# A decoder layer's gate projection, computed inside the scan loops, kept in DRAM and reloaded

## The reference

```
xz = norm(x) @ W_in ; xp, z = split(xz)          # 512 + 512 channels
xc = silu(causal_conv(xp)) ; B, C = split(xc @ W_x) ; dt = softplus(xc @ W_dt + b)
h  = exp(dt * A) * h + dt * xc * B               # 16 states per channel
y  = sum over states (h * C) + D * xc
x  = x + (y * silu(z)) @ W_out                   # then attention, then experts
```

## Time and profile before

| what | value |
|---|---|
| median of 3 runs | 1635.24 us (1632.82 to 1635.37) |
| profiled execution, own time | 1633.4 us |
| its span | 1631.4 us |
| VectorE busy | 1405.1 us (86%) |
| TensorE busy | 1249.2 us (77%), weight loads 834.0 |
| GpSimd busy | 969.0 us (59%) |
| ScalarE busy | 931.2 us (57%) |
| mean granted TensorE clock | 0.891 |

### The profile page before, as it was taken

How to read it: one execution, slowest core, us unless ns; L and a number is a source line. 1 busy time by engine, 2 the same in 40 slices (tenths; PEclk the granted TensorE clock), 3 DMA queues, 4 the chain that set the end, 5 groups by cost and what they waited for, 6 DMA issues and landing times. The chain is left out here.

```text
span 1631.4 us, 22872 instructions
## 1 busy us (share of the span) xinstructions
PE 1249.2 (77%) x5502; PEld 834.0 (51%) x5558; DVE 1405.1 (86%) x1861; ACT 931.2 (57%) x1369; POOL 969.0 (59%) x529
## 2 busy tenths in 40 slices
PE   4766667898677767889777687898777677797797
PEld 2344444664455445565445455566345455565465
DVE  6599999796899999787799999888699999963687
ACT  2554444146777777334777767523777767612564
POOL 1399888213888889322798889430689888620000
PEclk9877787999798989999799989999789988997699
DMA  7111110202111111201111121021111111010111
GB/s 228 41 39 43 42 45 20 99 1 80 34 58 52 46 57 53 64 26 54 59 40 58 40 71 51 27 69 54 40 41 57 58 52 60 18 61 27 45 60 52
DMA packets 54633, 86.48 MB, mean 53 GB/s; under 512 B 8572, under 2 KB 35589, under 8 KB 54542
## 3 DMA queue, kind: packets, MB, share of 16 engines
q1 hardware_dynamic: 50972, 83.20, 15.3%
q10 hardware_dynamic: 3570, 2.21, 0.5%
HBM read 74.83 MB, written 10.57 MB: 52 GB/s over the span
## 5 line engine op out<-in xcount | busy, mean ns | idle before, releaser
L1692 PE MATMUL ps<-ident,work 128*128 128x128 f32 x1536 | 309.2, 324 | 247.6 <-DVE stage L1334 170.1
L1296 DVE TENSOR_TENSOR_SCAN work<-ps,work 128x1024 f32<-128x1024 f32 x192 | 438.3, 2283 | 18.1 <-ACT ps L917 10.2
L1692 PEld LDWEIGHTS ps<-ident,work 128*128 128x128 f32 x1536 | 188.5, 159 | 383.6 <-DVE stage L1334 221.6
L917 ACT ACTIVATE ps<-dt,a_neg 128x1024 f32<-128x1024 f32 x256 | 284.8, 1117 | 121.1 <-DVE work L1296 96.3
L672 POOL TENSOR_TENSOR work<-dtu,b_bc 128x1024 f32<-128x1024 f32 x128 | 299.1, 2365 | 46.8 <-PE ps L1692 43.0
L1334 DVE SCALAR_TENSOR_TENSOR stage<-ps,c_tok,stage 128x512 f32<-128x512 f32 x384 | 272.1, 733 | 22.2 <-PE ps L1692 19.7
L1714 PE MATMUL ps<-w,work 128*128 (+1 forms) x1024 | 269.5, 411 | 1.8 <-DVE work L1441 1.8
L1714 PEld LDWEIGHTS ps<-w,work 128*128 128x128 f32 x1024 | 216.3, 213 | 52.6 <-issue 10.2
L1664 PE MATMUL ps<-nfT,w 128*128 128x512 bf16 x456 | 155.1, 430 | 40.5 <-DVE work L1371 14.6
L672 POOL TENSOR_TENSOR work<-dtu,w_out 128x1024 f32<-128x1024 f32 x64 | 149.3, 2355 | 50.1 <-PE ps L1692 50.1
L688 POOL TENSOR_TENSOR stage<-stage,work 128x512 f32<-128x512 f32 x128 | 160.5, 1277 | 11.4 <-ACT work L933 11.4
(11 more groups left out here) (164 smaller groups left out, 1879.7 us busy)
## 6 DMA issues: line engine op xcount, KB each, us to landing
b_bc<-b_rows SPq DMA_DIRECT2D x32, 512.0 KB, 3.7
w_out<-b_rows SPq DMA_DIRECT2D x32, 512.0 KB, 3.9
wbc<-combine_rows SPq DMA_DIRECT2D x64, 256.0 KB, 3.3
stage<-in_x SPq DMA_DIRECT2D x8, 512.0 KB, 4.1
xt<-in_x SPq DMA_DIRECT2D x8, 512.0 KB, 5.8
x_rows<-xt SPq DMA_DIRECT2D x4, 1024.0 KB, 4.2
res<-x_rows SPq DMA_DIRECT2D x8, 512.0 KB, 4.0
out_x<-res SPq DMA_DIRECT2D x8, 512.0 KB, 3.3
```

The source lines that it names most:

```text
L917: act.activation(decay_in(d, alone, opening), dt[:, d, :], ACT.Exp, scale=a_neg[:, bass.ds(it * 2 + (d * N + hf * (N // 2) + par), 1)]).th ...
L1296: dve.tensor_tensor_scan(h, decays, h, 0.0, ALU.mult, ALU.add).then_inc(scan_done, 1)
L1692: mm = pe.transpose(ps[:, a % HT_BANKS, d * P:(d + 1) * P], slot(par, d)[:, a * P:(a + 1) * P], ident[:, :])
```

## The change

- Z products move from the head into the scan loops: one per two states (`z_product`: 128 tokens, 8 matmuls into bank 0 after tile 6 is accumulated; the second state of each pair in the first eight states, the first state of each pair in the last eight). ScalarE copies the result to SBUF (`keep_z`), SP stores it to a DRAM tensor `zd` (`store_z`). In loops with experts the copy lands in `mix`.
- When state 14 is transposed, SP loads both halves back (`load_head`) into `soft`, where the slots of state 14 were.
- ScalarE's second linear relu goes behind the next state's first decay in the states that keep a Z (`late_linear`). The second down product goes into the state after (`late_down`).
- At the end of a row the accumulates, gates, Y transposes, skips and gated products are interleaved, and the second finalize stands partly among them (`gate`, `skip`, `gated_product`). ScalarE stores the second half of the output.
- In state 9 the finalize moves behind scan 1 and behind scan 2. Its three adds become scalar_tensor_tensor with a multiplication by 1.
- PSUM banks of the jobs are listed by hand (`banks_of`), GpSimd's gated products move to the end of its loop, and the key bias is loaded after the last Y is taken. `phase_after(b)` is the phase that follows loop b.

The diff, cut to its core (indentation shortened by eight columns):

```diff
...
+def z_job(b, hf, it):
+    return b * TT + hf * ITS + it
...
     def phases(ph):
         r, b = ph.c_row, ph.a_row
         if r is not None:
-            wait_apart(sp, dbu_ready, (r + 1) * (N * CT) + DBU_CREDIT)
-            wait_apart(sp, hT_ready, (r + 1) * (N * TT) + HT_READY_CREDIT)
-            sp.dma_start(w_out[:, :, :].rearrange("p k n -> p (k n)"), w_outd).then_inc(w_out_loaded, 16)
-            load_x(r, xt, [xt_loaded, xt_loaded])
-            sp.dma_start(key_bias.rearrange("p (o f) -> p o f", o=1),
-                         k_rowd[bass.ds(r, 1), :].partition_broadcast(P)).then_inc(key_bias_loaded, 16)
             sp.dma_start(kq[:, :, :], kqd[bass.ds(r * P, P), :].rearrange("p (k f) -> p k f", k=DK)
                          ).then_inc(kv_loaded, 16)
             sp.dma_start(vo[:, :, :], vod[bass.ds(r * KEYS, KEYS), :].rearrange("p (k f) -> p k f", k=2)
...
+            ph.wait_taken(sp, ("Y", CT - 1, NH - 1))
+            sp.dma_start(key_bias.rearrange("p (o f) -> p o f", o=1),
+                         k_rowd[bass.ds(r, 1), :].partition_broadcast(P)).then_inc(key_bias_loaded, 16)
         if r is not None:
             ph.wait_taken(sp, ("V", TT - 1, 0))
...
-        def loads(hf, first, last, opening=False):
+        def store_z(hf, it):
+            wait_apart(sp, z_kept, z_job(b, hf, it) + 1)
+            sp.dma_start(zd[:, :, bass.ds(it * P + hf * HALF, P)], z_kept_in[bp is not None]
+                         ).then_inc(z_stored, 16)
+        def load_head():
+            wait_apart(sp, dbu_ready, (b + 1) * (N * CT) + DBU_CREDIT)
+            sp.dma_start(w_out[:, :, :].rearrange("p k n -> p (k n)"), w_outd).then_inc(w_out_loaded, 16)
+            wait_apart(sp, hT_ready, (b + 1) * (N * TT) - TT + HT_READY_CREDIT)
+            for c in halves:
+                wait_apart(sp, z_stored, z_job(b, c, ITS) * 16 + Z_CREDIT)
+                sp.dma_start(soft[:, c * CT:(c + 1) * CT, :], zd[:, :, c * HALF:(c + 1) * HALF]
+                             ).then_inc(z_loaded[c], 16)
+            wait_apart(sp, hT_ready, (b + 1) * (N * TT) + HT_READY_CREDIT)
+            load_x(b, xt, [xt_loaded, xt_loaded])
+        def loads(hf, first, last, opening=False, turning=False):
...
                     if b is not None and not opening:
                         load_b(b, hf, it, par)
+                        if hf == 0 and par == 0:
+                            store_z(0, it - 1)
+                        if turning and par == 0:
+                            store_z(0, ITS - 1)
+                        if hf == 1 and par == 1:
+                            store_z(1, it)
...
-        loads(1, 0, 2)
+        loads(1, 0, 1, turning=True)
+        loads(1, 1, 2)
...
-        if bp is not None:
+        if b is None:
             store_out(1)
         else:
+            load_head()
+        if bp is None:
...
         turns(pool, body)
+        add_evicted(1, ITS, 0)
         if bp is not None:
             weigh(1, ITS, 0)
-        add_evicted(1, ITS, 0)
+        ph = phase_after(b)
+        for c in halves:
+            for d in range(CT // 2):
+                ph.wait_taken(pool, ("Y", d, c))
+                cols = slice(c * HALF, (c + 1) * HALF)
+                pool.tensor_tensor(xc[:, d, cols], xc[:, d, cols], dt[:, d, cols],
+                                   ALU.mult).then_inc(gated[0], 1)
...
+        def keep_z(hf, it):
+            n = z_job(b, hf, it)
+            wait_apart(act, z_stored, n * 16 + Z_CREDIT)
+            wait_apart(act, z_ready, n + 1)
+            act.activation(z_kept_in[bp is not None], ps[:, 0, :].rearrange("p (d t) -> p d t", d=CT), ACT.Copy
+                           ).then_inc(z_kept, 1)
+        def gate_tanhs(c, tiles):
+            wait_apart(act, z_loaded[c], b * 16 + 16)
+            for d in tiles:
+                act.activation(dt[:, d, c * HALF:(c + 1) * HALF], soft[:, c * CT + d, :], ACT.Tanh,
+                               scale=0.5).then_inc(gate_tanh, 1)
+        def late_linear(hf, it, par):
+            bank = ps[:, LINEAR_BANK, :]
+            turning = isinstance(it, int) and it * 2 + par == 0
+            col = 4 * E - 1 if turning else it * 8 + (par * 4 - 1)
+            wait_apart(act, p1_ready, state(bp, hf, it, par) * 4)
+            act.activation(bank, bank, ACT.Relu, scale=-1.0, bias=bias1[:, bass.ds(col, 1)]
+                           ).then_inc(both_linear, 1)
         def linear_in(hf, it, par, j):
...
                 return
             if bp is None or not (hf == 0 and isinstance(it, int) and it == 0):
                 decay(b, bp is None, hf, it, par, 0)
+            turning = hf == 1 and isinstance(it, int) and it == 0
+            if bp is not None and (par == hf or turning):
+                late_linear(hf, it, par)
             evict(hf, it, par)
...
                 chains[1][1]()
+            if par == 1 - hf:
+                keep_z(hf, it)
+            elif bp is not None:
                 linear_in(hf, it, par, 1)
...
             turns(act, body)
+        gate_tanhs(0, range(2))
         evict(1, ITS, 0)
         if bp is not None:
             clip(state(bp, 1, ITS, 0) * 2)
+        gate_tanhs(0, range(2, CT))
+        gate_tanhs(1, range(CT))
+        if bp is not None:
+            wait_apart(act, out_ready, bp * 2 + 2)
+            act.dma_start(out_rows[bass.ds(bp * S + HALF, HALF), :].rearrange("(a p) d -> p a d", p=P),
+                          res[:, :, :]).then_inc(out_stored, 16)
...
                 dve.wait_ge(res_loaded, (bp * 2 + hf) * 16 + 16)
+                if b is not None:
+                    wait_apart(dve, z_stored, (z_job(b, 1, 0) + 1 if hf == 0 else z_job(b, 1, ITS)) * 16
+                               + Z_CREDIT)
...
-                dve.tensor_tensor(mix[:, :], mix[:, :], flat16, ALU.add).then_inc(mix_added, 1)
+                dve.scalar_tensor_tensor(mix[:, :], mix[:, :], 1.0, flat16, ALU.mult, ALU.add
+                                         ).then_inc(mix_added, 1)
...
-                dve.tensor_tensor(flat[:, first_half], mix[:, first_half], flat[:, first_half], ALU.add)
+                dve.scalar_tensor_tensor(flat[:, first_half], mix[:, first_half], 1.0, flat[:, first_half],
+                                         ALU.mult, ALU.add)
...
+        def gate(c, tiles):
+            cols = slice(c * HALF, (c + 1) * HALF)
+            for d in tiles:
+                wait_apart(dve, gate_tanh, b * CT * NH + c * CT + d + 1)
+                dve.scalar_tensor_tensor(dt[:, d, cols], dt[:, d, cols], 1.0, soft[:, c * CT + d, :],
+                                         ALU.add, ALU.mult)
+        def skip(ph, c):
+            cols = slice(c * HALF, (c + 1) * HALF)
+            for d in range(CT):
+                job = ("Y", d, c)
+                ph.wait_mm(dve, job)
+                dve.scalar_tensor_tensor(xc[:, d, cols], xc[:, d, cols], chan[:, 2, d:d + 1],
+                                         ph.bank(job), ALU.mult, ALU.add).then_inc(dve_freed, 1)
+        def gated_product(ph, c):
+            cols = slice(c * HALF, (c + 1) * HALF)
+            for d in range(CT // 2, CT):
+                ph.wait_taken(dve, ("Y", d, c))
+                dve.tensor_tensor(xc[:, d, cols], xc[:, d, cols], dt[:, d, cols],
+                                  ALU.mult).then_inc(gated[1], 1)
         def gate_product(s, j):
...
                 if after:
                     gate_product(s - 1, 1)
                 linear_product(s - 1, 1 - par, 1)
-            if bp is not None and second:
-                finalize(0, 0)
-                finalize(0, 1)
             scan(w, par, 1, decay_in(1, bp is None))
             accumulate(hf, it, par, 4)
             accumulate(hf, it, par, 5)
             if bp is not None:
                 gate_product(s, 0)
                 if second:
-                    finalize(0, 2)
+                    finalize(0, 0)
+                    finalize(0, 1)
             scan(w, par, 2, decay_in(2, bp is None))
             accumulate(hf, it, par, 6)
             if bp is not None:
                 linear_product(s, par, 0)
                 if second:
-                    finalize(0, 3)
+                    for part in range(2, 5):
+                        finalize(0, part)
             scan(w, par, 3, decay_in(3, bp is None))
             accumulate(hf, it, par, 7)
             if bp is not None:
                 gate_product(s, 1)
-                if second:
-                    finalize(0, 4)
...
             turns(dve, body)
+            ph = phase_after(b)
+            gate(0, range(2))
             if bp is not None:
                 linear_product(state(bp, 1, ITS, 0) - 1, 1, 1)
-            for a in range(EVICTED, TT):
+            for a in range(EVICTED, 6):
                 accumulate(1, ITS, 0, a)
+            gate(0, range(2, CT))
+            skip(ph, 0)
+            for a in range(6, TT):
+                accumulate(1, ITS, 0, a)
+            gated_product(ph, 0)
```

(61 more changed lines are left out.)

77 lines of the change are left out of this document (36 added, 41 removed).

## The result

The change makes the kernel faster by 0.6%: 1625.45 us (median of 7 runs, 1624.16 to 1629.8) against 1636.06 (7 runs on the same chip, 1632.82 to 1640.21), ratio 0.9939, 95% interval 0.9925 to 0.9952. 1621.7 us was predicted. The profiled execution took 1627.51 us with a span of 1625.7, against 1633.4 and 1631.4 before.

A forecast was written before the change was run, and what follows sets the result against it. The prediction took VectorE to bound the loops and TensorE's chain the row ends. Its terms, -30.0 + 3 + 6 + 7 + 0.5 = -13.5 us, took 1635.24 to 1621.7 us; range for 8 in 10: 1604 to 1638.

The forecast's parts named there:

- Row ends, -30.0: Four stretches behind the last scans: Z products leave TensorE's chain, VectorE then sets the time; -30.0 us in all.
- Row 3's -11.5: End of row 3, with no next row's norm: last O product added by 30.5 us against 42.3, -11.5 us.
- Late down product at nothing: Down products moved one state on fit TensorE's idle time or are covered by the scan; no cost.
- Reload: Load of the Z tiles at row ends: 4.2 to 5.5 us, there when the last scan ends, no further wait.
- Z in rows 1 to 3, +3: Z products in these loops delay VectorE 0.7 us at the low clock, 18% of 24 states: +3 us.
- Z in row 0, +6: Z products and their copy ahead of the decay in row 0's loop: eight states at 0.75 us, +6 us.
- Finalize, +7: Finalize inside the loop, rows 1 to 3: three adds each wait 1.2 us for GpSimd, +2.3 a row, +7 us.
- My rival that took the rule at a whole GpSimd product for each step, +4.3 a row: Finalize in the loops: three steps wait for three GpSimd products, +4.3 us a row, 1627.7 us; chance 0.12.
- Tail, +0.5: Last three finalize steps at the kernel's end, GpSimd idle: +0.5 us for the bf16 step.
- No exclusion: Finalize's new form doesn't exclude GpSimd and Z is cheap: finalize gives 4 us, 1610.7 us; chance 0.28.
- Z holds up the decay: ScalarE's copy of Z ahead of the next decay costs 33 us instead of 9: 1645.7 us; chance 0.14.
- Reload late: Z tiles arrive 4 us late at four row ends: 1637 us, no measurable change; chance 0.10.

The follow-up runs named there:

- 1: The changed kernel with the stores of the folded weights in row 0 issued before all reloads at the row's end: 1625.5 us, ratio 0.9929.
- 5: The changed kernel with row 0's stores of the folded weights issued between the reloads of the gate (Z) products and of x: 1618.16 us, ratio 0.9888.
- 3: The changed kernel with ScalarE's copy of the gate (Z) product in row 0 put behind the next state's first decay: 1617.95 us, ratio 0.9883.
- 7: The changed kernel with each gate (Z) product cut to one matmul instead of eight, leaving work out: 1623.31 us, ratio 0.992.
- 2: The changed kernel with finalize's three adds back to tensor_tensor at their new places: 1617.99 us, ratio 0.988.
- 8: The kernel before the change with finalize's three adds as scalar_tensor_tensor at their old places: 1638.69 us, ratio 1.001.
- 4: The changed kernel with finalize's adds apart (ahead of scan 2, ahead of scan 3, at the state's end), still scalar_tensor_tensor: 1616.91 us, ratio 0.9866.
- 11: The changed kernel with rows 1 to 3 written out instead of a loop over them: 1618.42 us, ratio 0.9889.

## Why the prediction was right where it was, and wrong where not

- **Row ends, -30.0, measured -24.1.** Row 3's -11.5 was right (-12.6 with its tail). Its mechanism is right throughout: VectorE sets these stretches, T waits for it. What failed is the path through SyncE's queue. The sentence that SP's later loads have 5 us or more before anyone needs them names the key rows alone, and row 0 was taken as "the same without experts". That held in rows 1 and 2. In row 0 the stores of the folded weights stand in the same queue, and I had not followed what they are moved behind. 5.28 us, shown by 1 and 5. In rows 1 and 2 the forecast left out the late down product at the low clock (1.92 and 0.47 us, against 0.2 for TensorE in the sum) and the 1.90 us at the loop's head. The kernel before has 1.88 us of it, hidden behind TensorE's Z products; with these gone it is on the path.
- **Late down product at nothing** was wrong at the row's end; in the loops no run prices it apart.
- **Reload.** The first half lands 5.4 us after its issue, at the edge of my 4.2 to 5.5, the second after 7.2 to 7.9. At row 1 ScalarE waits 0.84 us for the first tanh, inside the slack that I had given it. At row 0 the states are shorter, and VectorE waits 1.85 us for that tanh; the forecast, which had put the second accumulate of row 0 1.9 us later, in part for the reload, covered it.
- **Z in rows 1 to 3, +3.** Some 0.8 us a row outside the finalize's pair of states, 2.4. Right.
- **Z in row 0, +6, measured +4.7.** Near by luck: two errors that offset. Each of the eight states loses 1.1 us, not 0.75, as the copy stands ahead of the decay (3) and the product takes 2.05 us, not 1.5: I had counted one weight load for each of the eight matmuls, and the trace has two. The six others behind the first gain 0.5 each, at the higher clock (7), which I had named but counted only in the states with a product.
- **Finalize, +7, measured +10** (3.3 to 3.4 a row). The reason was right, the size too small. The forecast let all three adds wait because both forms read two SBUF operands, and 2 and 8 show both forms waiting alike. But it took 1.2 us a wait from adds at other places. Here the three steps take 6.9 us (1.40, 2.71, 2.82) instead of 6.2, and the state after grows by 0.5, which the forecast did not have. The place sets the size, three adds in a row inside GpSimd's products (4). The rule of the Trainium skill that I had cited (page SBUF — State Buffer, section Who interferes with whom) says just this, whatever the opcode: two SBUF inputs on VectorE contend with GpSimd's reads. The runs agree, with 2.71 and 2.82 us for adds that take 0.68 alone. My rival that took the rule at a whole GpSimd product for each step, +4.3 a row, was as near as my own term, and its 1627.7 us nearer than my 1621.7.
- **Tail, +0.5**: 1.21 for 0.68. Right.
- **The rivals.** No exclusion: refuted by the adds from 568.81 to 572.88. Z holds up the decay: this is what happens in row 0, at 1.1 us a state, but over the 32 states it is 0.34 us ((8.6 + 2.4) / 32), half of the 0.7 from which it decides. Reload late: not by 4 us at any row, but by 1.6 at row 0, and 1 shows what more would cost, with the stores ahead of it.

What stays open is why one late down product or another meets the low clock; it moves row ends by 1 to 4 us between kernels that don't differ there, and with it part of the gain of 2 and 11.

## What to carry to other kernels

When a load is moved ahead in a queue that issues in order, list what it is moved past and what waits behind these, for each row apart: the first one may have work that the others lack. Work in the gaps of the bound engine costs by its place: a VectorE add with both inputs in SBUF belongs where GpSimd is idle, and a copy ahead of a decay only where the decay can wait. A stretch that TensorE bounded hides stalls of other engines that appear once TensorE is out of the way.
